# Scattering the first experts' output rows to token order, and loading them plainly in the second attention stage

## The reference, cut to what matters

```python
x = x + L0_attention(layernorm(x), ctx)      # stage A
x = x + L0_experts(layernorm(x))             # stage B, no capacity limit
x = x + L1_attention(layernorm(x), ctx)      # stage C
x = x + L1_experts(layernorm(x))             # stage D, capacity 640 tokens an expert
```

```python
probs = softmax(xf @ router_w.T); top_w, top_idx = top_k(probs, 2)
h = silu(einsum('td,efd->tef', xf, w1)); y = einsum('tef,edf->ted', h, w2)
out = einsum('te,ted->td', combine, y * expert_scale)
```

## Time and profile before

| what | value |
|---|---|
| time, median of three runs | 1435.98 us (1431.56 to 1443.38) |
| time of the profiled execution | 1428.03 us |
| its span, first to last instruction | 1426.0 us |
| mean granted TensorE clock | 0.969 |
| PE busy | 1325.1 us (93%) |
| DVE, ACT, POOL busy | 863.9, 824.4, 683.4 us (61%, 58%, 48%) |
| HBM read, written | 93.44 MB, 31.97 MB |

### The profile page before, as it was taken

One profiled execution on the slowest core, in us unless ns is written; L12 is line 12 of the kernel. 1 busy time (PEld: TensorE's weight loads), 2 busy tenths in 40 slices (PEclk: granted clock), 3 DMA queues, 4 the chain that ended last, 5 costly groups with the idle time before them and its releaser, 6 DMA issues.

```text
span 1426.0 us, 37828 instructions
## 1 busy us (share of the span) xinstructions
PE 1325.1 (93%) x13044; PEld 1083.4 (76%) x13044; DVE 863.9 (61%) x2396; ACT 824.4 (58%) x1946; POOL 683.4 (48%) x939
## 2 busy tenths in 40 slices
PE   6999999998689999999997899999983999999997
PEld 5787778786556666666665899999972899999996
DVE  5787888887533333233232688888864666666664
ACT  4787878876255555555552666666642455555543
POOL 4335656555633333333331557777746344444423
PEclk9999999999699999999999999999996999999999
DMA  5345444543189999999995233333312555554541
GB/s 149 96 126 123 117 114 103 124 93 65 39 145 181 205 179 173 177 174 177 181 168 137 79 90 91 93 100 96 94 52 63 154 145 141 145 147 130 136 127 54
DMA packets 299962, 177.58 MB, mean 125 GB/s; under 512 B 232094, under 2 KB 278400, under 8 KB 299780
## 3 DMA queue, kind: packets, MB, share of 16 engines
q1 hardware_dynamic: 278196, 140.44, 44.6%
q0 software_dynamic: 18608, 32.21, 8.7%
q10 hardware_dynamic: 2976, 2.52, 0.7%
HBM read 93.44 MB, written 31.97 MB: 88 GB/s over the span
## 4 chain that ended last, share of the span: by engine, by line
PE 81%; DVE 6%; ACT 4%; issue 4%; DMA 2%; POOL 1%; another core or an unknown queue 0%; ACTq 0%; SPq 0%; DVEq 0%; POOLq 0%
PE psum L2448 15%; PE psum L1476 13%; PE psum L1496 13%; PE psum L2465 7%; PE psum L1997 4%; PE psum L1987 2%; PE psum L902 2%; PE psum L1946 2%; PE psum L1907 2%; PE psum L831 2%; PE psum L1913 2%; DVE mx L1052 2%; PE psum L844 2%; PE psum L905 2%; PE psum L919 2%
## 5 line engine op out<-in xcount | busy, mean ns | idle before, releaser
L2448 PE MATMUL psum<-d_xT,d_w 128*128 128x256 f16 (+1 forms) x2304 | 222.1, 255 | 1.0 <-issue 1.0
L1396 DVE SCALAR_TENSOR_TENSOR b_h<-b_hid,b_h 128x1024 f16<-128x1024 f32 x71 | 87.0, 1225 | 212.0 <-ACT b_h L1431 212.0
L2448 PEld LDWEIGHTS psum<-d_xT,d_w 128*128 128x128 f16 x2304 | 198.9, 98 | 20.1 <-issue 1.1
L1496 PE MATMUL psum<-arena,b_hT 128*128 x1704 | 200.8, 275 | 6.0 <-DMA b_hT<-b_h 5.8
L1476 PE MATMUL psum<-arena,b_xT 128*128 x852 | 197.7, 382 | 7.4 <-DMA b_xT<-b_x 6.0
L1496 PEld LDWEIGHTS psum<-arena,b_hT 128*128 128x128 f16 x1704 | 167.3, 99 | 43.6 <-issue 9.4
L1306 POOL DMA_INDIRECT b_xg<-dram_normed,b_gi x71 | 69.1, 974 | 207.0 <-issue 153.7
L1476 PEld LDWEIGHTS psum<-arena,b_xT 128*128 128x128 f16 x852 | 83.7, 98 | 97.2 <-issue 12.6
L2531 ACT ACTIVATE d_sg<-psum 128x256 f32<-128x256 f32 (+1 forms) x192 | 66.2, 347 | 153.4 <-PE psum L2448 150.3
L2597 DVE SCALAR_TENSOR_TENSOR d_hf<-psum,d_sg 128x256 f32<-128x256 f32 (+1 forms) x192 | 71.7, 379 | 93.9 <-ACT d_sg L2531 82.2
L1424 ACT ACTIVATE b_hid<-psum 128x512 f32<-128x512 f32 x142 | 83.4, 596 | 64.8 <-PE psum L1476 56.4
(11 more groups left out here) (331 smaller groups left out, 2969.7 us busy)
## 6 DMA issues: line engine op xcount, KB each, us to landing
d_wst<-in_L_w SPq DMA_DIRECT2D x64, 384.0 KB
stage<-in_L_w SPq DMA_DIRECT2D x32, 512.0 KB, 4.6
dram_expert_rows<-b_ys SPq DMA_DIRECT2D x71, 128.0 KB
ctxT<-in_ctxT SPq DMA_DIRECT2D x64, 128.0 KB, 3.5
dram_normed<-xn SPq DMA_DIRECT2D x64, 128.0 KB
x<-in_x SPq DMA_DIRECT2D x32, 128.0 KB, 4.0
dram_x<-xnew SPq DMA_DIRECT2D x32, 128.0 KB
c_x<-dram_x SPq DMA_DIRECT2D x32, 128.0 KB
```

The costliest lines, as they stand in the source:

```text
L1396: dve.scalar_tensor_tensor(out=h16[:, p, 1, :], in0=hid[:, p, :], scalar=H_SCALE, in1=h16[:, p, 0, :], op0=ALU.mult, op1=ALU.subtract).the ...
L1496: i = pe.matmul(psum[:, 6 + p, 0:D], hT[:, p, ph_, c, :], weights(e, 2 + c // 4, pw, (c % 4) * D, D), start=(n == 0), stop=(n == len(terms ...
L2448: i = pe.matmul(psum[:, q, m * n:(m + 1) * n], w16[:, fc % RING, pw, col:col + P], xT[:, p, px, c, at:at + n], start=(k == 0), stop=(k == ...
```

## The change

Stage B no longer stores the experts' rows in slot order. POOL scatters them by an indirect DMA to row 2t + k of a table in token order, so that stage C reads the two rows of each of 128 tokens as one plain block of 256 KB.

For this the second number of a table row is no longer the token again but 2t + k. `pairs` becomes a tile with both numbers for k = 0 and 1, made by two iotas; `no_token` becomes T and 2T in turn, so unused slots are all written to the same spare row 2T. The row numbers of a block are now read twice, at the gather and at the scatter 6 blocks later, so `gi` has 12 buffers. What served the old order goes: `slots` and its copy in each group of stage A, `of_slots` on DVE, the cast in `scaled`, SP's store, and the gathers of stage C.

```diff
-        ys_d = dram("expert_rows0", (BLOCKS0 * P, D))
+        ys_d = dram("token_rows0", (2 * T + 1, D))
...
-                pool.iota(no_token[:, :], pattern=[[0, 2 * (SPARE0 + P) // P]], base=T, channel_multiplier=0)
+                pool.iota(no_token[:, :], pattern=[[0, (SPARE0 + P) // P], [T, 2]], base=T, channel_multiplier=0)
...
-                pool.iota(pairs[:, :, :], pattern=[[P, NB], [0, 2]], base=0, channel_multiplier=1)
+                pool.iota(pairs[:, :, :, 0:1].rearrange("p b k a -> p b (k a)"), pattern=[[P, NB], [0, 2]], base=0, channel_multiplier=1)
+                pool.iota(pairs[:, :, :, 1:2].rearrange("p b k a -> p b (k a)"), pattern=[[2 * P, NB], [1, 2]], base=0, channel_multiplier=2)
...
-                                            pairs[:, b, :], None, bounds_check=bound, oob_is_err=False).then_inc(scat[g % 4], 16)
+                                            pairs[:, b, k, :], None, bounds_check=bound, oob_is_err=False).then_inc(scat[g % 4], 16)
...
-                        dve.wait_ge(slots_kept, g)
+                        dve.wait_ge(slot_ready, g)
...
-                    dve.tensor_copy(slots[:, first:first + n, :].rearrange("p j k -> p (j k)"), gslot[:, 2 * at:2 * to]).then_inc(slots_kept, 1)
...
-            NX, NT = 6, 4
+            NX, NT, NI = 6, 4, 12
...
-                        if due(j - NX + 1):
-                            pool.wait_ge(g_ld[j % NX], nth(j - NX, NX))
-                        pool.indirect_dma_start(gi[:, j % NX, :], None, ids[0], bass.IndirectOffsetOnAxis(ap=ypos[:, j:j + 1], axis=0)
+                        if due(j - NI + 1):
+                            pool.wait_ge(y_st[j % 2], nth(j - NI))
+                        pool.indirect_dma_start(gi[:, j % NI, :], None, ids[0], bass.IndirectOffsetOnAxis(ap=ypos[:, j:j + 1], axis=0)
...
+                def put(j):
+                    if inside(j):
+                        pool.wait_ge(y_ready, j + 1)
+                        if due(j):
+                            pool.wait_ge(y_st[(j - 1) % 2], nth(j - 1))
+                        pool.indirect_dma_start(ys_d, bass.IndirectOffsetOnAxis(ap=gi[:, j % NI, 1:2], axis=0), ys[:, j % 2, :], None
+                                                ).then_inc(y_st[j % 2], 16)
...
                 for j in range(N_B):
                     gather(j)
                     load_ids(j + 2)
+                    put(j - NX)
...
                 scaled(pool)
+                for j in range(N_B - NX, N_B):
+                    put(j)
...
                 for j in range(-4, N_B):
                     low_h(j + 1)
                     low_x(j + 4)
-                    if j == 2:
-                        of_slots(dve)
...
-                    store(j - 2)
...
-                pool.tensor_copy(gi[:, :, :], slots[:, :, :])
...
+            def load_y(sp, b):
+                if inside(b):
+                    if due(b - NY + 1):
+                        sp.wait_ge(x2_ready, b - NY + 1)
+                    sp.dma_start(yg[:, b % NY, :, :].rearrange("p k d -> p (k d)"), ys_d[2 * P * b:2 * P * (b + 1), :].rearrange("(p k) d -> p (k d)", k=2)
+                                 ).then_inc(yg_ld[b % NY], 16)
...
+                for b in range(NY):
+                    load_y(sp, b)
                 load_x1(sp, 2)
                 for b in range(NB + 2):
                     if b == NB:
                         first_weights(sp)
                     load_x1(sp, b + 3)
+                    load_y(sp, b + NY)
...
-                gather(0)
-                gather(1)
                 norm1(0)
-                gather(2)
                 norm1(1)
-                gather(3)
                 for b in range(NB + 4):
                     norm2(b - 2)
                     for c in turn.get(b, ()):
                         scatter(*c)
                     norm1(b + 2)
-                    gather(b + 4)
```

More of the change, by code:

```diff
@@ L112, in build @@
         routew = sb("routew", [P, NB, 2])
-        slots = sb("slots", [P, NB, 2])
+        pairs = sb("pairs", [P, NB, 2, 2], I32)
         carry = sb("carry", [P, E])
@@ L352, in first_attention @@
             lg_done, top_steps, top_done, hot_steps, hot_ready = (psem(n) for n in ("lg_done", "top_steps", "top_done", "hot_steps", "hot_ready"))
-            cnt_done, cnt_read, slot_steps, slot_ready, slots_kept = (psem(n) for n in (
-                "cnt_done", "cnt_read", "slot_steps", "slot_ready", "slots_kept"))
+            cnt_done, cnt_read, slot_steps, slot_ready = (psem(n) for n in ("cnt_done", "cnt_read", "slot_steps", "slot_ready"))
             d8_ready, e8_ready, prob_ready, sec_ready, w_steps, w_ready = (psem(n) for n in (
@@ L1364, in of_blocks @@
                 dve.tensor_scalar(ypos[:, r], aj[:, r], float(SPARE0), pcol[:, 0:1], ALU.add, ALU.add).then_inc(t_ready, 1)
-            def of_slots(dve):
-                k = tsteps
-                sl = slots[:, :, :].rearrange("p b k -> p (b k)")
-                dve.tensor_copy(lim[:, 0:1], base[:, 0:1])
-                dve.tensor_tensor(lim[:, 1:E], base[:, 1:E], base[:, 0:E - 1], ALU.subtract).then_inc(t_steps, 1)
-                dve.wait_ge(t_steps, k.next())
-                dve.tensor_scalar(base[:, :], regions[:, 0, :], 1.0, None, ALU.add).then_inc(t_steps, 1)
-                dve.wait_ge(t_steps, k.next())
-                dve.tensor_tensor(ygt[:, :, :], cols(sl, E), rows(base[:, :], 2 * NB), ALU.is_ge).then_inc(t_steps, 1)
-                dve.wait_ge(t_steps, k.next())
-                dve.tensor_tensor(ygt[:, :, :], ygt[:, :, :], rows(lim[:, :], 2 * NB), ALU.mult).then_inc(t_steps, 1)
-                dve.wait_ge(t_steps, k.next())
-                dve.tensor_reduce(ysl[:, :], ygt[:, :, :], AX.X, ALU.add).then_inc(t_steps, 1)
-                dve.wait_ge(t_steps, k.next())
-                dve.tensor_tensor(sl, sl, ysl[:, :], ALU.subtract).then_inc(t_steps, 1)
-                dve.wait_ge(t_steps, k.next())
             def b_dve(dve):
@@ L1533, in transpose_h @@
                                                h16[:, p, :, :].rearrange("p h f -> p (h f)")).then_inc(hT_ld[p], 16)
-                def store(j):
-                    if inside(j):
-                        sp.wait_ge(y_ready, j + 1)
-                        sp.dma_start(tile(ys_d, j), ys[:, j % 2, :]).then_inc(y_st[j % 2], 16)
                 for j in range(-3, N_B + 2):
                     transpose_h(j)
-                    store(j - 2)
                     transpose_x(j + 3)
@@ L1709, in c_pool @@
                 bound = pool.to_reg(SPARE1 - 1)
-                def gather(b):
-                    if inside(b):
-                        if b == 0:
-                            pool.wait_ge(c_cast, 1)
-                        if due(b - NY + 1):
-                            pool.wait_ge(x2_ready, b - NY + 1)
-                        for k in range(2):
-                            pool.indirect_dma_start(yg[:, b % NY, k, :], None, ys_d, bass.IndirectOffsetOnAxis(ap=gi[:, b, k:k + 1], axis=0)
-                                                    ).then_inc(yg_ld[b % NY], 16)
                 def norm1(b):
@@ L2072, in add_experts @@
                         x, rw = x6[:, b % 6, :], routew[:, b, :]
-                        dve.wait_ge(yg_ld[b % NY], 2 * nth(b, NY))
+                        dve.wait_ge(yg_ld[b % NY], nth(b, NY))
                         dve.wait_ge(x_ld[b % 6], nth(b, 6))
```

6 lines of the change are left out of this document (2 added, 4 removed).

## The result

The changed kernel takes 1452.09 us (median of five runs, 1442.87 to 1456.19), the kernel before, run beside it, 1436.52 (five runs, 1431.56 to 1443.38): a ratio of 1.0099, 95% interval 1.0071 to 1.0126. The change costs 1%. The profiled execution took 1442.87 us, with a span of 1441.2 and a mean granted clock of 0.973, where that of before took 1428.03: 14.8 us more, about what the medians say. Stage B alone is 12.3 of it, and its rows may be read for the loss.

A forecast was written before the change was run, and what follows sets the result against it. PE was taken to bound stages B and C, with DMA engines nearly full in B. Terms +0.2 - 0.3 - 0.5 + 0 + 0.9 - 0.5 = -0.2 us on 1428.03 gave 1427.8, plus 8.0 to the median: 1436; range 1425 to 1449.

The forecast's parts named there:

- chain of puts in B: Stage B: each put waits for the last one's landing, taken as 3.3 us; period 4.6 us, nothing waits: 0.
- SP's store gone, POOL's issue in its place: Stage B: transposes behind SP's store can be issued about a microsecond sooner; -0.5 us (0 to -4).
- scattered rows instead of a plain block: Stage B: same bytes, 128 KB a block in rows of 1 KB, on POOL's queue; DMA load taken as unchanged.
- stage C and the seam by plain loads: Between stages B and C +0.9 us (-0.8 to +4.5); in stage C -0.5 us (0 to -4).
- the seam: From stage B's last store to DVE's start in C: 6.6 us before, 7.5 after; +0.9 (-0.8 to +4.5).
- tables and slots: One more iota at the start, +0.2 us; stage A's DVE copies gone, -0.3; of_slots was hidden, worth nothing.
- rival 1: Stage B: POOL waits for the last put's landing, next gather behind it; 1449 to 1484 us, likeliest 1458; chance 0.17.
- deciding value at 4.0: Stage B: a put must land within 4.0 us of its building's end, else B runs at the put's pace.
- Stage C: Stage C: POOL loses 2.5 us a block but frees nobody but ACT, bound 3.6 us; -0.5 us (0 to -4).
- rival 2: Stage C speeds up if POOL's turns lengthen its seven long blocks; with other stalls about 13 us, 1423; chance 0.13.
- Rival 3: Between B and C: unused slots' writes to one spare row queue up, last put lands late; 1441 to 1444; chance 0.12.

The follow-up runs named there:

- first set: Changed kernel without the wait between puts, unused slots skipped: 1.0023; same with the wait: 1.0103; kernel before with only stage C's plain loads: 0.9961; only B's scatter: 1.0123.
- third set: SP's wait for y_ready put back into three kernels: plain store from POOL 0.9996; unchained scatter with gather released earlier 0.9993; changed kernel with gather released earlier 1.0092.
- fifth set: Kernel before with stage C's plain loads 0.9956; also B's plain store issued by POOL 1.0000; also SP's wait for y_ready 1.0008; changed kernel, unchained, unused slots skipped 1.0023.
- fourth set: Changed kernel again 1.0081; with B's gather of x released one block earlier 1.0162; with that and SP's wait for y_ready kept 1.0117.
- early gather: B's gather of x released one block earlier; in the changed kernel 1.0010, repeated 1.0162; in the kernel before 0.9996.
- B half: Changed kernel with stage C's two indirect gathers a block put back, by row numbers 2t + k: 1.0123, 1448.79 us.
- C half: Kernel before with stage C's two gathers a block replaced by one plain 256 KB load on SP, slot-order table, other tokens' rows: 0.9961, repeated 0.9956.
- scattered free kernel: Changed kernel with no put waiting for the put before it and unused slots skipped by a bound: 1.0023, 1432.23 us; repeated 1.0023, 1431.61 us.
- second set: Gather of x released one block earlier in the unchained kernel 1.0017, changed kernel 1.0010, kernel before 0.9996; stage C's plain loads with B's plain store from POOL 1.0015.

## Why the prediction was wrong

It gave 1436 us, with a range up to 1449; the time is 1452.09. The sum by its own steps (the changed kernel's ratio of 1.0099 is 14 us):

| part | forecast, us | measured, us |
|---|---|---|
| chain of puts in B | 0 | +11 to +14 (first set, third set) |
| SP's store gone, POOL's issue in its place | -0.5 | +6 (fifth set) |
| scattered rows instead of a plain block | 0 | +2 to +3, not resolved (fifth set) |
| stage C and the seam by plain loads | +0.4 | -4 to -6 (first and fifth set) |
| tables and slots | -0.1 | within the +2 to +3 |
| sum | -0.2 | +13 to +19 |

**The puts in B: the step that failed.** The prediction had the mechanism, its condition and its price as rival 1, and left it there because it took 3.3 us for a put's landing, "nearer to D", with the deciding value at 4.0. Measured are 5.5 us for the put at 543.23, and 3.5 to 6.3, in the mean 5.2, from the end of building to the next put's start over all that waited. Two terms were mis-sized. The landing was taken from stage D's scatter (2.57), a quieter stage (a DMA share of 0.54 around it), over the two gathers of the very stage (4.35 and 4.74; in the changed kernel one took 6.60 from its issue), by the argument that the put is issued when the h transposes are mostly through. That can hold at best for a put that is on time; in the bunch each is late, and the argument has nothing to say of them. And the restart after a landing was taken as the usual 0.30; the chain's rows show 0.76 (549.74 to 550.50). So what decides is a landing of 5.27 - 1.00 - 0.76 = 3.5 us, not 4.0. The prediction misread its row for D here: the 2.57 end at POOL's next start, so they hold the restart already. Like with like, from the end of building to POOL's next start, D has 2.57 and B's eleven waiting puts 5.2, where a block allows 5.27 - 1.00 = 4.27.

The Trainium skill ("DMA: Bandwidth & Descriptors", Latency and other measured facts) had spoken for the late landing: it puts most of a transfer's fixed cost in the receipt from the target memory and lets HBM access grow from 0.2 to 2 us under load. The trace agrees in direction: 5.5 us at a share of 0.98, and 3.12 - 0.97 = 2.2 us for the last put at the seam, when the transposes are over and the share is 0.09. The same instruction with the same bytes lands in less than half the time. The load is not all that differs, since the last blocks' slots are mostly unused and their rows go to the spare row.

**The price of rival 1.** "65 x (period - 5.27)" would have given +60 us at 6.2. It was +12, because only eleven of the puts in the steady part waited. The loss came in a bunch, from 485 to 628 us, with the pace of 5.26 after it. The rival's 1449 to 1484 hold the result, but its price took every block for a waiting one.

**The way in which the chain costs.** "With the gather behind it" was half of it. In the changed kernel it is so: ACT waited 133.9 us for x instead of 91.6. But the third and fourth set show that an early gather does not save it, since `ys` is late then. "y_out(j) needs put(j - 2) landed: 7 us after" was right for one put alone; it left out that a put is itself late when the one before is.

**SP's store.** Forecast as -0.5, since nobody waits for SP. Moving it to POOL's queue cost 6 us. In "the bytes are the same [...] so I take the DMA load as unchanged" the conclusion fails: on POOL's queue the same bytes take 2.7 points of the DMA engines' time instead of 1.7, in a stage whose DMA share was 0.95 to begin with. That this is why PE loses is not shown. The order on SP costs nothing (1.0008 beside 1.0000), as forecast.

**Tables, slots, `of_slots`.** Nothing shows against them: with its B half and C half taken apart, the scattered free kernel leaves 2 to 3 us for all of them and the scattering together, not resolved.

**The seam.** Forecast 7.5 us from `y_out`'s end to DVE; measured 0.29 + 3.12 + 0.02 + 2.57 + 0.03 = 6.0 (783.98 to 790.01). The put's landing there was right (2.2 for 2.0), the load of 256 KB was 2.57 where 3.9 was taken from page medians of loads under load.

**Stage C.** The usual block stayed at 8.28 us and the long one at 9.09 (923.36 to 932.45), where 8.6 would have been the sign of rival 2. ACT's wait for POOL fell from 3.6 to 2.2 us only, PE's for ACT rose from 4.6 to 6.2: POOL had held nobody, as forecast, and rival 2 fails. The Trainium skill ("GPSIMD Engine Reference", Specifications) would have let DVE's long blocks shrink with less work on POOL; 15 us less of POOL in 50 shortened the stage by 2 us of 316, within what the traces differ by. C's half gained some 5 us all the same, 2 of them at the seam through one hop that POOL no longer makes; where the other 3 are is not resolved. The forecast counted the seam for the whole change only, and there the put takes most of that gain away again (from `y_out`'s end 6.6 us before, 4.5 with C's half alone, 6.0 in the changed kernel).

**The spare row.** Rival 3 gave 1441 to 1444, 5 to 8 us for the seam and the writes to one row; skipping those writes changed nothing that can be seen, and the seam came out shorter.

## What to carry to other kernels

A wait of one DMA for the landing of the last, on the queue of an engine that also issues loads, has to fit landing *and* restart into one period: price it with the slowest landing seen in the same stage (here 4.7 us for its gathers, and a put took 5.5), not with the same instruction in a quieter stage. If writes must not collide, make it impossible by their addresses (here: do not write the unused rows) instead of serialising them; that took back 0.8% in one set and 1.0% in another. And moving a transfer to another queue was not free here, where the DMA engines were 0.96 busy, even at equal bytes and with the engine that now issues it less than half busy: look at the share that the packets take on either queue.

## What was not expected of the hardware

- Landing of the same 128 KB scatter: 2.2 us after building at the end of B (its rows mostly going to the one spare row), 5.5 in the middle of it; in one trace 2.6 to 7.0 from the issue, median 4.6 (36 puts).
- A plain store of 128 KB issued by POOL is built in 0.58 us, and costs 6 us over 71 blocks against the same store issued by SP; it goes in 48 packets instead of 144.
- The same kernel, changed with early gather, stood at 1.0010 (0.9991 to 1.0029) beside the kernel before in one set and at 1.0162 (1.0129 to 1.0195) in another, and the kernel before itself moved from 1416.7 to 1438.4 us. A difference under 1% is to be read inside one set.
- In 415 to 755 us one kernel's POOL waited 38 times for a put, 82.8 us, and PE kept its pace (changed with early gather, second set); the changed kernel's waited 11 times, 24.8 us, and lost 2.4 blocks of PE's work. The sum of a wait on an engine that does not bound says little; what PE did in the same stretch says it.
